# A graph network's dense first layer: the ELU split over ScalarE and VectorE another way, its output a step later

## Chip, cores and metric

The kernel runs on one core of one Trainium2 chip. The metric is the device time of one execution in microseconds (us): 4633.51 us is the median of three runs of the kernel before (4628.96 to 4634.05).

## What is computed

The program is a chain of four graph layers over 50000 nodes of 128 features and 12500 edges. Only the first layer matters here, and of it the part that every node takes:

```python
def _L0_gnn_ref(x, edge_index, edge_attr, u, batch, W1a, b1a, W1b, b1b, W2a, b2a, W2b, b2b):
    ...
    agg = summed / jnp.maximum(counts, 1.0)[:, None]
    z = jnp.concatenate([x, agg], axis=1)
    return jax.nn.elu(z @ W2a + b2a) @ W2b + b2b

x = _layernorm(x + _L0_gnn_ref(x, edge_index, edge_attr_128, ...), axis=-1)
```

Most nodes receive no edge, so for them `agg` is zero and the layer is x + ELU(x W2a[0:128] + b2a) W2b + b2b, normalised over its 128 features. The kernel computes this "dense" form for all nodes; the nodes with edges are computed again in a later stage. ELU(v) is v for v > 0 and exp(v) - 1 otherwise.

## The kernel before

All engines follow one list, `plan` (L512 to L527), written in Python before any instruction is issued. Each engine calls its own function for each entry of the list (`follow`, L529), so every engine has its work in the same order, and semaphores carry the data from one to the other. The list mixes two jobs:

- **The sort of the edges.** Edges are taken in 26 groups of 512. `hist` (26 entries) counts keys: VectorE makes one-hot matrices in bf16 (L770, L771), TensorE multiplies them (L645). `table` makes running sums and a node table in DRAM. `rank` (112 entries, called slots here, four to a group of edges) finds each edge's place: GpSimd (POOL) issues two indirect gathers per slot (`note`, L594) and two indirect scatters per slot (`place`, L601), TensorE looks up and counts (L678, L664), ScalarE makes one-hots by square and rectified line (L732, L735, L746, L749), VectorE compares, extracts and matches (L771, L851, L855, L840).
- **The dense layer.** The nodes are taken in 98 groups g of 512, four nodes to a partition. The entry `dense k` is one step of a software pipeline; `staged(k - lag, NG, f)` calls f for group k - lag.

Thirteen dense steps lie between the `hist` entries (one after each two), two behind `table`, and the other 88 are spread over the 112 slots, so that about four slots of five have a dense step behind them.

What each engine does in dense step k, in its own order:

- SP: load x of group k+1 (`load_x`, waits until POOL has used that buffer), load the transposed x of group k+2 (`load_xt`), store the result of group k-5 (`store1`).
- TensorE: `out0` of group k-2 (L697, eight 128x128 products into the one bank OUT0), then `hidden` of group k (L690, two products of 512 columns into two of three banks HB). `out0` waits for VectorE's `residual1` of group k-3, since there is one OUT0 bank, and VectorE does that in the same step k.
- ScalarE: `scale1` of group k-4 (L720, four normalising activations), then `exps` of group k (L712): exp(HB + b2a) into `hid1`, two activations of 128x512.
- VectorE: `shift` of group k-4 (L876), `elu_low` of group k-1 (L905), `residual1` of group k-3 (L882), `elu_high` of group k-1 (L910, two instructions), then `stats1`, `moments`, `eps` of group k-3 (L888, L895, L901).
- POOL: `add_bias` of group k-1 (L621, x + b2b into `xb`; waits for `residual1` of group k-3), then `power` of group k-3 (L627, the power -0.5 of the variance; waits for `eps` of group k-3, same step).

The ELU is done by these two functions of VectorE:

```python
def elu_low(g):
    after(dve, expd, g)
    nc.vector.tensor_scalar(hid1[g % 2][:, :, :], hid1[g % 2][:, :, :], 1.0, -1.0, MIN, ADD).then_inc(tmin, 1)

def elu_high(g):
    after(dve, tmin, g)
    for h in range(2):
        nc.vector.scalar_tensor_tensor(hid1[g % 2][:, h, :], HB[(2 * g + h) % 3][:, :], bias[h], hid1[g % 2][:, h, :], ADD, MAX).then_inc(elud, 1)
```

`after(eng, sem, g)` lets an engine wait until `sem` has been raised g+1 times. `hid1` and `xb` lie in SBUF, HB and OUT0 in PSUM. `after`, `after_ring` and `staged` are at L141 to L162, the block's LAST (the number of dense steps, 103) at L506.

Of the kernel before, what the change touches and what calls it, by code (L numbers as in the profile page):

```python
# [21 lines left out]
P = 128  # L22
# [142 lines left out]
def build(nc, a, out):  # L165
    ctx = ExitStack()
    with ctx:
# [53 lines left out]
        b2b_bc = sb("b2b_bc", [P, J, D])  # L221
        WL1 = sb("WL1", [P, D])
# [36 lines left out]
        hid = hid2[0]  # L259
        agg = [sb(f"agg{u}", [P, 2, GR]) for u in range(2)]  # L260
# [80 lines left out]
        with nc.Block() as block:  # L341
# [81 lines left out]
            def _(dve):  # L423
# [12 lines left out]
                nc.vector.tensor_tensor(b0[:, 6:8], b0[:, 4:6], B[0][:, 0:2], ADD).then_inc(floats, 1)  # L436
                dve.wait_ge(tpe, 3)
# [4 lines left out]
                dve.wait_ge(floats, 6)  # L442

            @block.tensor
            def _(pe):
                pe.wait_ge(made, 1)
                pe.wait_ge(raw_st, 1)
                for f in range(7):
                    if f >= 2:
                        pe.wait_ge(tpe, f - 1)  # L450
                    if f == 0:
# [6 lines left out]
                        for c in range(2):  # L458
                            for q in range(2):
                                last = nc.tensor.matmul(B[0][:, c:c + 1], W2a[:, 1 + q, c * P:(c + 1) * P], b0[:, 2 + q:3 + q],  # L460
                                                        start=(q == 0), stop=(q == 1))
                        last.then_inc(wf_p, 1)
# [6 lines left out]
         hidd, expd, tmin, elud, xbd, y1d, r1d, st1d, mvd, epsd, powd, shd, x1d) = ph.sems(33)  # L469
# [29 lines left out]
        HB, OUT0 = [PS[4], PS[5], PS[7]], PS[6]  # L499
        xd = [*x2N[0], spare_x]  # L500
        xt = [agg[u][:, h, :] for u in range(2) for h in range(2)]
        hid1 = hid2[0]
# [3 lines left out]
        LAST = NG + 5  # L506
# [33 lines left out]
        with nc.Block() as block:  # L540

            @block.sync
            def _(sp):
# [28 lines left out]
                def dense(k):  # L572
                    staged(k + 1, NG, load_x)
                    staged(k + 2, NG, load_xt)
                    staged(k - 5, NG, store1)

                load_x(0)
# [7 lines left out]
            def _(pool):  # L585
# [32 lines left out]
                def add_bias(g):  # L618
                    after_ring(pool, x_in, g, 16)
                    after(pool, r1d, g - 2)  # L620
                    nc.gpsimd.tensor_tensor(flat(xb[g % 2]), flat(xd[g % 3]), flat(b2b_bc), ADD).then_inc(xbd, 1)  # L621
# [16 lines left out]
            def _(pe):  # L638
# [47 lines left out]
                def hidden(g):  # L686
                    after_ring(pe, xt_in, g, 16)
                    for h in range(2):
                        after(pe, elud, 2 * g + h - 3)
                        nc.tensor.matmul(HB[(2 * g + h) % 3][:, :], W2a[:, 0, h * P:(h + 1) * P], xt[g % 4], start=True, stop=True).then_inc(hidd, 1)  # L690

                def out0(g):
                    after(pe, elud, 2 * g + 1)
                    after(pe, r1d, g - 1)
                    for j in range(J):
                        for c in range(2):
                            last = nc.tensor.matmul(OUT0[:, spans[j]], hid1[g % 2][:, c, spans[j]], W2b[:, c, :], start=(c == 0), stop=(c == 1))  # L697
# [9 lines left out]
            def _(act):  # L707
                def exps(g):
                    after(act, y1d, g - 2)
                    for h in range(2):  # L710
                        after(act, hidd, 2 * g + h)
                        last = nc.scalar.activation(hid1[g % 2][:, h, :], HB[(2 * g + h) % 3][:, :], ACT.Exp, bias=bias[h])  # L712
                    last.then_inc(expd, 1)
# [9 lines left out]
                def dense(k):  # L723
                    staged(k - 4, NG, scale1)
# [34 lines left out]
            def _(dve):  # L759
# [118 lines left out]
                def residual1(g):  # L878
# [3 lines left out]
                    nc.vector.tensor_tensor(flat(r1[g % 2]), OUT0[:, :], flat(xb[g % 2]), ADD).then_inc(r1d, 1)  # L882
# [20 lines left out]
                def elu_low(g):  # L903
                    after(dve, expd, g)
                    nc.vector.tensor_scalar(hid1[g % 2][:, :, :], hid1[g % 2][:, :, :], 1.0, -1.0, MIN, ADD).then_inc(tmin, 1)  # L905

                def elu_high(g):
                    after(dve, tmin, g)
                    for h in range(2):
                        nc.vector.scalar_tensor_tensor(hid1[g % 2][:, h, :], HB[(2 * g + h) % 3][:, :], bias[h], hid1[g % 2][:, h, :], ADD, MAX).then_inc(elud, 1)  # L910

                def dense(k):
                    staged(k - 4, NG, shift)
                    staged(k - 1, NG, elu_low)
                    staged(k - 3, NG, residual1)
                    staged(k - 1, NG, elu_high)
# [2336 lines left out]
```

## Time and profile before

| what | value |
|---|---|
| median of three runs | 4633.51 us |
| lowest, highest | 4628.96, 4634.05 us |
| the profiled execution, its own time | 4636.57 us |
| span of the profiled execution | 4634.4 us |
| mean granted TensorE clock | 0.916 |
| busy: PE, DVE, ACT, POOL | 3559.5, 3407.8, 2211.6, 3222.0 us |

The block that the change touches runs from about 36 us to 1000 us of the span: `hist` with its dense steps until about 165 us, `table` until about 184 us, then the slots. Blocks are one after the other, with all engines meeting at each end. Engines: PE is TensorE, PEld its weight load, DVE is VectorE, ACT is ScalarE, POOL is GpSimd, SP is the queue of plain transfers. A row of grouped instructions has busy time, mean duration in ns, then the idle time of the engine just before them and what ended it. A row of a timeline has start and duration in us; the bracket is idle time before it and what ended that. Neighbouring VectorE instructions overlap a little in their recorded times, so the pitch from start to start is the cost of one.

### The profile page before, as it was taken

How to read it: one execution, taken by the hardware profiler on the slowest of the kernel's cores; microseconds unless marked ns; L12 is line 12 of the kernel's file. 1: busy time of each engine (PE TensorE's matmuls, PEld its weight loads, DVE VectorE, ACT ScalarE, POOL GpSimd, SP SyncE). 2: the span in 40 equal slices, each digit the busy share in tenths (PEclk: the TensorE clock that was granted, in tenths of full speed). 3: DMA queues.
4: the chain of work that ended last, by engine and by line, in shares of the span. 5: the costliest groups of instructions: out<-in, count | busy, mean ns of one | idle time of the engine just before them, and what ended most of it. 6: DMA issues, size and time to landing. Idle time of an engine off the chain costs nothing. (4 is left out here: it accounts for less than half of the span.)

```text
span 4634.4 us, 61427 instructions
## 1 busy us (share of the span) xinstructions
PE 3559.5 (77%) x14977; PEld 2219.4 (48%) x14977; DVE 3407.8 (74%) x10458; ACT 2211.6 (48%) x4450; POOL 3222.0 (70%) x2802
## 2 busy tenths in 40 slices
PE   5677777747777566489979999998688758687975
PEld 3465555534444466444435555554343357564321
DVE  7777877755666688755546888888766669797964
ACT  1366666632333477623327777777122313123742
POOL 1377878757777588677747888888588766462557
PEclk9888989879999787799989999999899979898988
DMA  3344444432333467534433333333333258695863
GB/s 92 95 126 117 123 116 128 121 99 80 96 96 91 130 205 208 170 114 140 135 112 107 125 125 125 125 125 117 102 109 107 86 178 254 160 193 144 279 197 111
DMA packets 463592, 621.19 MB, mean 134 GB/s; under 512 B 71541, under 2 KB 220204, under 8 KB 463308
## 3 DMA queue, kind: packets, MB, share of 16 engines
q1 hardware_dynamic: 402700, 534.09, 37.1%
q0 software_dynamic: 54912, 83.37, 8.3%
q8 instruction: 105, 1.72, 0.2%
q10 hardware_dynamic: 5696, 0.55, 0.1%
q14 instruction: 179, 1.47, 0.1%
HBM read 402.95 MB, written 218.46 MB: 134 GB/s over the span
## 5 line engine op out<-in xcount | busy, mean ns | idle before, releaser
L1180 PE MATMUL ps<-big,Whh 128*128 128x512 f32 x1176 | 540.1, 595 | 33.5 <-DVE big L1198 30.9
L697 PE MATMUL ps<-W2b,hid 128*128 128x128 f32 x1568 | 249.3, 326 | 197.6 <-DVE rN L882 197.6
L1605 PE MATMUL ps<-big,We 128*128 128x512 f32 x800 | 356.2, 599 | 5.0 <-DVE big L1755 3.8
L697 PEld LDWEIGHTS ps<-W2b,hid 128*128 128x128 f32 x1568 | 236.4, 236 | 234.9 <-issue 233.1
L1180 PEld LDWEIGHTS ps<-big,Whh 128*128 128x128 f32 x1176 | 212.2, 190 | 254.3 <-issue 251.4
L1213 POOL TENSOR_TENSOR big<-big 128x512 f32<-128x512 f32 x196 | 251.6, 1303 | 73.0 <-ACT big L1207 73.0
L712 ACT ACTIVATE hid<-ps,b 128x512 f32<-128x512 f32 x196 | 134.0, 686 | 300.0 <-PE ps L690 290.0
L594 POOL DMA_INDIRECT me<-node_tab,ix x208 | 217.4, 1045 | 72.7 <-issue 52.8
L1755 DVE SCALAR_TENSOR_TENSOR big<-r2N,zN 128x512 f32<-128x512 f32 x400 | 252.7, 685 | 16.2 <-DMA r2N<-type_row 6.4
L601 POOL DMA_INDIRECT meta<-me,rank_ix x208 | 214.1, 1030 | 63.1 <-issue 60.6
L1605 PEld LDWEIGHTS ps<-big,We 128*128 128x128 f32 x800 | 151.5, 192 | 188.3 <-issue 182.5
L1198 DVE SCALAR_TENSOR_TENSOR big<-ps,bhh,hid 128x512 f32<-128x512 f32 x196 | 142.4, 744 | 125.9 <-ACT hid L1191 119.7
L1223 POOL TENSOR_TENSOR big<-big 128x512 f32<-128x512 f32 x98 | 141.3, 1462 | 127.3 <-DVE big L1218 127.3
L1527 POOL DMA_INDIRECT xN<-h_tab,ix x100 | 169.9, 1699 | 56.5 <-issue 28.8
L1121 DVE TENSOR_SCALAR zN<-rN,moments,rstd 128x128 f32<-128x128 f32 x392 | 191.7, 561 | 22.6 <-POOL rstd L1109 22.6
L2716 POOL DMA_INDIRECT xN<-x_tab,ix x100 | 161.6, 1616 | 67.2 <-PE ps L2730 35.4
L690 PE MATMUL ps<-agg,W2a 128*128 128x512 f32 x392 | 206.5, 654 | 0.0
L1190 ACT ACTIVATE hid<-ps,brz 128x512 f32<-128x512 f32 x196 | 134.6, 687 | 137.8 <-PE ps L1180 132.5
L678 PE MATMUL ps<-big,hotrow 128*128 128x256 f32 x832 | 188.5, 380 | 5.7 <-ACT hotrow L735 5.7
L2746 PEld LDWEIGHTS ps<-big,hid 128*128 128x128 f32 x1600 | 187.5, 194 | 8.0 <-DVE hid L2865 1.5
L2746 PE MATMUL ps<-big,hid 128*128 128x128 f32 x1600 | 189.6, 277 | 1.1 <-DVE hid L2865 1.1
L2418 ACT ACTIVATE hid<-big,shq,rsq 128x128 f32<-128x128 f32 x392 | 160.5, 483 | 31.9 <-DVE shq L2525 31.9
(403 smaller groups left out, 10744.3 us busy)
## 6 DMA issues: line engine op xcount, KB each, us to landing
xN<-x_tab SPq DMA_DIRECT2D x196, 256.0 KB, 3.0
h_tab<-yN SPq DMA_DIRECT2D x124, 256.0 KB, 2.3
krow<-key_row SPq DMA_DIRECT2D x100, 256.5 KB, 4.3
agg<-in_xt SPq DMA_DIRECT2D x98, 256.0 KB, 3.2
big<-x_tab SPq DMA_DIRECT2D x98, 256.0 KB, 3.1
x_tab<-hid SPq DMA_DIRECT2D x98, 256.0 KB, 3.5
agg<-x_tab SPq DMA_DIRECT2D x98, 256.0 KB, 2.8
x_tab<-zN SPq DMA_DIRECT2D x98, 256.0 KB, 2.0
```

What stands on the lines that cost most here:

```text
L594: nc.gpsimd.indirect_dma_start(me[:, t, f:f + 4], None, node_tab, at_index(which, i, j)).then_inc(noted[i % 2].sem, 16)
L601: nc.gpsimd.indirect_dma_start(meta[k], bass.IndirectOffsetOnAxis(ap=rank_ix[:, k, t:t + 1], axis=0), me[:, t, :], None).then_inc(stored[k ...
L678: last = nc.tensor.matmul(LOOK[j // 2][:, (j % 2) * LO:(j % 2 + 1) * LO], hotrow[k][:, h, j * P:(j + 1) * P], R[:, k, h, :], start=(h == 0 ...
L690: nc.tensor.matmul(HB[(2 * g + h) % 3][:, :], W2a[:, 0, h * P:(h + 1) * P], xt[g % 4], start=True, stop=True).then_inc(hidd, 1)
L697: last = nc.tensor.matmul(OUT0[:, spans[j]], hid1[g % 2][:, c, spans[j]], W2b[:, c, :], start=(c == 0), stop=(c == 1))
L1121: last = nc.vector.tensor_scalar(self.y[u][:, j, :], self.r[u][:, j, :], self.mv[u][:, j, 0:1], self.rs[u][:, j, :], SUB, MUL)
L1180: last = nc.tensor.matmul(bank[:, :], Whh[:, l, c * D:(c + 1) * D], h, start=True, stop=not both)
L1213: nc.gpsimd.tensor_tensor(self.d[u], h[u], self.n[u], SUB).then_inc(self.dd, 1)
L1527: nc.gpsimd.indirect_dma_start(xs[u][:, j, :], None, x2_e if l == 0 else h1_tab, at_index(IX_X2SRC if l == 0 else IX_H1SRC, g + EDGE0, j)) ...
L1605: last = nc.tensor.matmul(MS[:, :], We[:, l * NTYPE + t, :], masked[g % 2][:, t, :], start=(t == 0), stop=(t == NTYPE - 1))
L1755: last = nc.vector.scalar_tensor_tensor(masked[u][:, t, :], types[u], float(t), hs[u], EQ, MUL)
L2746: last = nc.tensor.matmul(OUT[u][:, spans[j]], ranked[u][m][:, spans[j]], weightI[l][m], start=(m == 0), stop=(m == TOP - 1))
```

## The change

The ELU is computed as min(exp(v), 1) + max(v, 0), which is ELU(v) + 1. ScalarE makes both parts from PSUM, with a second activation (Relu) for each half into a new buffer `above`; VectorE joins them by one `scalar_tensor_tensor` over 1024 columns with both inputs in SBUF. The extra 1 is taken back through the bias: `b2b_less` is b2b minus the column sums of W2b, made once in the setup block by two products with a matrix of ones (TensorE) and four subtractions (VectorE). ELU buffers become three, output banks OUT0 two, hidden banks HB two. The join moves from step g+1 to g+2, `out0` from g+2 to g+3, `residual1`, `stats1`, `moments`, `eps` and `power` from g+3 to g+4, `shift` and `scale1` from g+4 to g+5, the store from g+5 to g+6; `add_bias` moves from g+1 to g+3 and its load from g-1 to g. LAST goes from 103 to 104, so 89 dense steps are spread over the 112 slots.

```diff
+        b2b_less = sb("b2b_less", [P, J, D])
+        hid3 = [sb(f"hid_c{u}", [P, 2, GR]) for u in range(2)]
...
                 nc.vector.tensor_tensor(b0[:, 6:8], b0[:, 4:6], B[0][:, 0:2], ADD).then_inc(floats, 1)
+                for j in range(J):
+                    last = nc.vector.tensor_tensor(b2b_less[:, j, :], b2b_bc[:, j, :], H[1][0][:, 0:D], SUB)
+                last.then_inc(floats, 1)
...
+                        for c in range(2):
+                            last = nc.tensor.matmul(H[1][0][:, 0:D], ones[:, :], W2b[:, c, :], start=(c == 0), stop=(c == 1))
                         last.then_inc(wf_p, 1)
...
-        HB, OUT0 = [PS[4], PS[5], PS[7]], PS[6]
+        HB, OUT0 = PS[4:6], PS[6:8]
-        hid1 = hid2[0]
+        hid1, above = [*hid2[0], hid3[0]], [*hid2[1], hid3[1]]
-        LAST = NG + 5
+        LAST = NG + 6
...
                 def dense(k):
-                    staged(k + 1, NG, load_x)
+                    staged(k, NG, load_x)
                     staged(k + 2, NG, load_xt)
-                    staged(k - 5, NG, store1)
+                    staged(k - 6, NG, store1)
...
-                    nc.gpsimd.tensor_tensor(flat(xb[g % 2]), flat(xd[g % 3]), flat(b2b_bc), ADD).then_inc(xbd, 1)
+                    nc.gpsimd.tensor_tensor(flat(xb[g % 2]), flat(xd[g % 3]), flat(b2b_less), ADD).then_inc(xbd, 1)
...
                 def dense(k):
-                    staged(k - 1, NG, add_bias)
-                    staged(k - 3, NG, power)
+                    staged(k - 3, NG, add_bias)
+                    staged(k - 4, NG, power)
...
                     for h in range(2):
-                        after(pe, elud, 2 * g + h - 3)
-                        nc.tensor.matmul(HB[(2 * g + h) % 3][:, :], W2a[:, 0, h * P:(h + 1) * P], xt[g % 4], start=True, stop=True).then_inc(hidd, 1)
+                        after(pe, reld, 2 * g + h - 2)
+                        nc.tensor.matmul(HB[h][:, :], W2a[:, 0, h * P:(h + 1) * P], xt[g % 4], start=True, stop=True).then_inc(hidd, 1)
 
                 def out0(g):
-                    after(pe, elud, 2 * g + 1)
-                    after(pe, r1d, g - 1)
+                    after(pe, elud, g)
+                    after(pe, r1d, g - 2)
...
                 def dense(k):
-                    staged(k - 2, NG, out0)
+                    staged(k - 3, NG, out0)
                     staged(k, NG, hidden)
...
                 def exps(g):
-                    after(act, y1d, g - 2)
+                    after(act, y1d, g - 3)
+                    after(act, elud, g - 3)
                     for h in range(2):
                         after(act, hidd, 2 * g + h)
-                        last = nc.scalar.activation(hid1[g % 2][:, h, :], HB[(2 * g + h) % 3][:, :], ACT.Exp, bias=bias[h])
-                    last.then_inc(expd, 1)
+                        nc.scalar.activation(hid1[g % 3][:, h, :], HB[h][:, :], ACT.Exp, bias=bias[h])
+                        nc.scalar.activation(above[g % 3][:, h, :], HB[h][:, :], ACT.Relu, bias=bias[h]).then_inc(reld, 1)
...
-                    staged(k - 4, NG, scale1)
+                    staged(k - 5, NG, scale1)
                     staged(k, NG, exps)
...
-                def elu_low(g):
-                    after(dve, expd, g)
-                    nc.vector.tensor_scalar(hid1[g % 2][:, :, :], hid1[g % 2][:, :, :], 1.0, -1.0, MIN, ADD).then_inc(tmin, 1)
-
-                def elu_high(g):
-                    after(dve, tmin, g)
-                    for h in range(2):
-                        nc.vector.scalar_tensor_tensor(hid1[g % 2][:, h, :], HB[(2 * g + h) % 3][:, :], bias[h], hid1[g % 2][:, h, :], ADD, MAX).then_inc(elud, 1)
+                def elu(g):
+                    after(dve, reld, 2 * g + 1)
+                    nc.vector.scalar_tensor_tensor(hid1[g % 3][:, :, :], hid1[g % 3][:, :, :], 1.0, above[g % 3][:, :, :], MIN, ADD).then_inc(elud, 1)
 
                 def dense(k):
-                    staged(k - 4, NG, shift)
-                    staged(k - 1, NG, elu_low)
-                    staged(k - 3, NG, residual1)
-                    staged(k - 1, NG, elu_high)
-                    staged(k - 3, NG, stats1)
-                    staged(k - 3, NG, moments)
-                    staged(k - 3, NG, eps)
+                    staged(k - 5, NG, shift)
+                    staged(k - 2, NG, elu)
+                    staged(k - 4, NG, residual1)
+                    staged(k - 4, NG, stats1)
+                    staged(k - 4, NG, moments)
+                    staged(k - 4, NG, eps)
```

VectorE, one dense step among the slots, between an extract (L851, L855; in the change L858, L862) and what follows. Before:

```order
L855 TENSOR_TENSOR big<-big,ps 128x512 [waits odd14]
...
L876 SCALAR_TENSOR_TENSOR shq<-mvq,rsq 128x4 [waits odd32,odd30]
L905 TENSOR_SCALAR hid<-hid 128x1024 [waits odd21]
L882 TENSOR_TENSOR rN<-ps,xb 128x512 [waits odd32,odd24,odd25]
L910 SCALAR_TENSOR_TENSOR hid<-ps,b,hid 128x512 [waits odd22]
L910 SCALAR_TENSOR_TENSOR hid<-ps,b,hid 128x512
L888 BN_STATS stats<-rN 128x6 [waits odd28,odd26]
```

In the change:

```order
L862 TENSOR_TENSOR big<-big,ps 128x512 [waits odd14]
...
L883 SCALAR_TENSOR_TENSOR shq<-mvq,rsq 128x4 [waits odd31,odd29]
L912 SCALAR_TENSOR_TENSOR hid_c<-hid_c 128x1024 [waits odd21]
L889 TENSOR_TENSOR rN<-ps,xb 128x512 [waits odd31,odd23,odd24]
L895 BN_STATS stats<-rN 128x6 [waits odd27,odd25]
```

The three ELU instructions have become one of 1024 columns, directly behind `shift` (L883), and nothing stands between `residual1` and `stats1` now.

POOL, the first dense instructions, in the `hist` part. Before (L621 is `add_bias`, L627 is `power`):

```order
L621 TENSOR_TENSOR xb<-xN,b2b_bc 128x512 x2
L621 TENSOR_TENSOR xb<-spare_x,b2b_bc 128x512
L627 TENSOR_TENSOR rsq<-veq,mhalf 128x4
L621 TENSOR_TENSOR xb<-xN,b2b_bc 128x512
L627 TENSOR_TENSOR rsq<-veq,mhalf 128x4
```

In the change (L627 is `add_bias`, L633 is `power`):

```order
L627 TENSOR_TENSOR xb<-xN,b2b_less 128x512 x2
L633 TENSOR_TENSOR rsq<-veq,mhalf 128x4
L627 TENSOR_TENSOR xb<-spare_x,b2b_less 128x512
L633 TENSOR_TENSOR rsq<-veq,mhalf 128x4
L627 TENSOR_TENSOR xb<-xN,b2b_less 128x512
```

The two alternate as before, but an `add_bias` no longer waits for a `residual1` of its own step: the one that it waits for was done a step earlier.

## Rows read from the trace of the kernel before

**Rows 1.** The page's part on busy time, whole program.

```profile
span 4634.4 us, 61427 instructions
PE 3559.5 (77%) x14977; PEld 2219.4 (48%) x14977; DVE 3407.8 (74%) x10458; ACT 2211.6 (48%) x4450; POOL 3222.0 (70%) x2802
```

**Rows 2.** Busy time by stretch: length, then PE, PEld, DVE, ACT, POOL, granted clock, DMA.

```profile
36.00:155.00 119.00, 91.51 (x591) 60.75 (x592) 117.50 (x518) 28.30 (x54) 24.20 (x22) 1.00 0.24 77
220.00:900.00 680.00, 523.59 (x2545) 404.33 (x2544) 542.84 (x2063) 447.62 (x805) 539.86 (x502) 0.89 0.44 122
937.00:1000.00 63.00, 39.42 (x214) 31.14 (x212) 42.89 (x173) 32.75 (x64) 42.30 (x40) 0.88 0.24 73
```

**Rows 3.** Waits of 220 to 900 us: who for whom, us, times, longest.

```profile
ACT hid L712 <- PE ps L690: 195.3, 72, 5.2
PE ps L697 <- DVE rN L882: 154.3, 43, 5.6
DVE hid L905 <- ACT hid L712: 51.7, 38, 3.0
POOL rsq L627 <- DVE veq L901: 25.0, 28, 1.4
POOL xb L621 <- DVE rN L882: 9.9, 6, 2.1
```

**Rows 4.** Groups of instructions, 220 to 900 us.

```profile
L594 POOL DMA_INDIRECT me<-node_tab,ix x185 | 193.7, 1047 | 48.7 <-issue 46.9 <-DMA me<-node_tab,ix 0.9 <-ACT yN L720 0.6
L601 POOL DMA_INDIRECT meta<-me,rank_ix x173 | 178.7, 1033 | 52.7 <-issue 50.6 <-ACT yN L720 0.9 <-DVE rank_ix L866 0.6
...
L712 ACT ACTIVATE hid<-ps,b 128x512 f32<-128x512 f32 x144 | 98.3, 686 | 202.5 <-PE ps L690 195.3
...
L627 POOL TENSOR_TENSOR rsq<-veq,mhalf 128x4 f32<-128x4 f32 x72 | 77.6, 1078 | 27.7 <-DVE veq L901 25.0
```

**Rows 5.** POOL's indirect DMAs singly, 220 to 900 us: shortest, median, longest ns.

```profile
L594 POOL DMA_INDIRECT me<-node_tab,ix x185: 941/987/1506, 219.4 to 898.3; - x185
L601 POOL DMA_INDIRECT meta<-me,rank_ix x173: 982/998/1505, 258.2 to 899.6; - x173
```

**Rows 6.** Timeline of POOL, one slot with its dense step.

```profile
554.38 1.49 POOL L594 DMA_INDIRECT me<-node_tab,ix  x1 [0.20 <-issue]
556.17 0.97 POOL L594 DMA_INDIRECT me<-node_tab,ix  x1 [0.30 <-issue]
...
559.77 1.28 POOL L621 TENSOR_TENSOR xb<-xN,b2b_bc 128x512 f32<-128x512 f32 x1
561.00 1.04 POOL L627 TENSOR_TENSOR rsq<-veq,mhalf 128x4 f32<-128x4 f32 x1
562.23 1.50 POOL L594 DMA_INDIRECT me<-node_tab,ix  x1 [0.20 <-issue]
```

**Rows 7.** Timeline of VectorE in the same slot.

```profile
562.07 0.16 DVE L876 SCALAR_TENSOR_TENSOR shq<-mvq,rsq 128x4 f32<-128x4 f32 x1 [3.00 <-POOL rsq L627]
562.15 0.69 DVE L905 TENSOR_SCALAR hid<-hid 128x1024 f32<-128x1024 f32 x1
```

**Rows 8.** Timeline, POOL and VectorE, an edge match (L840) against an indirect DMA.

```profile
217.68 1.41 POOL L594 DMA_INDIRECT me<-node_tab,ix  x1 [0.19 <-issue]
...
217.46 0.75 DVE L840 SCALAR_TENSOR_TENSOR big<-xT,ef,mask 128x512 f32<-128x512 f32 x1
```

**Rows 9.** Timeline of VectorE, a dense step among the `hist` entries.

```profile
150.62 0.68 DVE L905 TENSOR_SCALAR hid<-hid 128x1024 f32<-128x1024 f32 x1
151.22 0.68 DVE L882 TENSOR_TENSOR rN<-ps,xb 128x512 f32<-128x512 f32 x1
151.82 1.40 DVE L910 SCALAR_TENSOR_TENSOR hid<-ps,b,hid 128x512 f32<-128x512 f32 x2
153.14 0.86 DVE L888 BATCH_NORM_STATS2 stats<-rN 128x6 f32<-128x128 f32 x4
```

**Rows 10.** Timeline, POOL's `add_bias` against VectorE's one-hots in `hist`.

```profile
45.20 1.29 POOL L621 TENSOR_TENSOR xb<-xN,b2b_bc 128x512 f32<-128x512 f32 x1 [1.75 <-DMA xN<-in_x]
...
45.22 1.36 DVE L771 TENSOR_SCALAR big<-iota_lo,ef 128x256 bf16<-128x256 bf16 x1
46.50 0.28 DVE L770 TENSOR_SCALAR big<-iota_lo,ef 128x256 bf16<-128x256 bf16 x1
```

**Rows 11.** A join of two SBUF inputs elsewhere in the program, and output products.

```profile
L2854 DVE SCALAR_TENSOR_TENSOR yN<-krow,spare_win 128x512 f32<-128x512 f32 x34 | 23.3, 684 | 0.0
...
L697 PE MATMUL ps<-W2b,hid 128*128 128x128 f32 x1568 | 249.3, 326 | 197.6 <-DVE rN L882 197.6
```

More of the change, by code:

```diff
@@ L441, in _ @@
                 nc.vector.memset(inv_e[:, :], 1.0).then_inc(floats, 1)
-                dve.wait_ge(floats, 6)
+                dve.wait_ge(floats, 7)
             @block.tensor
@@ L468, in build @@
         (hoth, histd, cum, tot, off, offs, start_, tabs, own_d, has_d, map_d, hot, hotT, looked, counted, based, eqd, radd, base_w, ranked,
-         hidd, expd, tmin, elud, xbd, y1d, r1d, st1d, mvd, epsd, powd, shd, x1d) = ph.sems(33)
+         hidd, reld, elud, xbd, y1d, r1d, st1d, mvd, epsd, powd, shd, x1d) = ph.sems(32)
         tab_st, mv_set, squared, squared_hi, hot_hi = ph.sems(5)
@@ L572, in dense @@
                 def dense(k):
-                    staged(k + 1, NG, load_x)
+                    staged(k, NG, load_x)
                     staged(k + 2, NG, load_xt)
-                    staged(k - 5, NG, store1)
-                load_x(0)
+                    staged(k - 6, NG, store1)
                 load_xt(0)
@@ L688, in hidden @@
                     for h in range(2):
-                        after(pe, elud, 2 * g + h - 3)
-                        nc.tensor.matmul(HB[(2 * g + h) % 3][:, :], W2a[:, 0, h * P:(h + 1) * P], xt[g % 4], start=True, stop=True).then_inc(hidd, 1)
+                        after(pe, reld, 2 * g + h - 2)
+                        nc.tensor.matmul(HB[h][:, :], W2a[:, 0, h * P:(h + 1) * P], xt[g % 4], start=True, stop=True).then_inc(hidd, 1)
                 def out0(g):
-                    after(pe, elud, 2 * g + 1)
-                    after(pe, r1d, g - 1)
+                    after(pe, elud, g)
+                    after(pe, r1d, g - 2)
                     for j in range(J):
                         for c in range(2):
-                            last = nc.tensor.matmul(OUT0[:, spans[j]], hid1[g % 2][:, c, spans[j]], W2b[:, c, :], start=(c == 0), stop=(c == 1))
+                            last = nc.tensor.matmul(OUT0[g % 2][:, spans[j]], hid1[g % 3][:, c, spans[j]], W2b[:, c, :], start=(c == 0), stop=(c == 1))
                     last.then_inc(y1d, 1)
                 def dense(k):
-                    staged(k - 2, NG, out0)
+                    staged(k - 3, NG, out0)
                     staged(k, NG, hidden)
@@ L881, in residual1 @@
                     after(dve, x1d, g - 2)
-                    nc.vector.tensor_tensor(flat(r1[g % 2]), OUT0[:, :], flat(xb[g % 2]), ADD).then_inc(r1d, 1)
+                    nc.vector.tensor_tensor(flat(r1[g % 2]), OUT0[g % 2][:, :], flat(xb[g % 2]), ADD).then_inc(r1d, 1)
                 def stats1(g):
```

## The prediction

> **What bounds the kernel now.** The page's busy times [rows 1] only say that no engine is alone in front: PE 77%, DVE 74%, POOL 70% of the whole program. The change touches one block of it, so I cut that block into stretches [rows 2]. In 36 to 155 us, the `hist` part, DVE is busy 117.5 of 119 us: it is the bound, and whatever it sheds there is gained. In 220 to 900 us, 92 slots with 72 dense steps, DVE is busy 543 of 680 us, PE 524, ACT 448 and POOL 540: nobody is full. Next I look at who waits for whom there [rows 3]. The large waits (ACT for `hidden` 195 us, PE for `residual1` 154 us, DVE for `exps` 52 us) form the ring that the change cuts. But POOL waits for DVE for only 25.0 + 9.9 = 34.9 us. The rest of its idle time stands in the groups [rows 4] as "issue": 46.9 + 50.6 us, the 0.3 us in front of each indirect DMA, which nothing shortens. So POOL works or issues for 680 - 34.9 = 645 us, 95% of the stretch. **POOL is the floor**, and cutting the ring between the others can give back 34.9 us there at most.
>
> One more thing must be read before the sum. An undelayed indirect DMA takes about 0.98 us, and some take 1.5 [rows 5]. The timeline shows when: POOL ends a `power`, DVE's `shift` was waiting for it and starts at 562.07, L905 follows at 562.15, and POOL's next DMA, begun at 562.23, lasts until 563.73, where the next ones take 0.97 [rows 6, 7]. L905 ended at 562.84. A DMA of that kind therefore waits for the end of a VectorE instruction that came before its own first access, and that costs it 0.48 us. It is the same with an instruction that has two SBUF inputs: the match that ran from 217.46 to 218.21 makes the DMA begun at 217.68 last 1.41 us [rows 8].
>
> **The change, part by part.**
>
> *Setup.* PE makes two more products ahead of the semaphore on which ACT and the transposes wait. Eight of them take 16 records; back to back one product costs about 0.25 us, and the mean record is 326 ns [rows 11]. I take **+0.5 us** (0.5 to 1.3). The four subtractions on DVE are small and fall into a wait for ACT; were that cover gone, they would cost about 1 us.
>
> *The hist part.* DVE sheds L905 (pitch 0.60) and two L910 (pitch together 1.32) [rows 9], 1.92 us in 12 steps = 23.0. It gains the join: 512 columns from two SBUF inputs take 684 ns [rows 11], of which some 0.15 us is fixed as between the pitches above, so 1024 columns have a pitch of 1.13 us (bounds: 1.05 and twice 0.68 = 1.37) in 11 steps = 12.4. A set of `residual1` to `eps` (2.0 us) leaves the part with the later step. With nothing between `residual1` and `stats1`, the semaphore shows, 0.12 us in 9 steps. In all 23.0 + 2.0 - 12.4 - 1.1 = 11.5 us less.
> But `add_bias` loses its cover. Before, it was released by `residual1` and ran under L910, which reads PSUM and one SBUF input and was not slowed. Now it follows the `power` of the step before at once and meets DVE's one-hots. The trace has that meeting: `add_bias` from 45.20 to 46.49, and the one-hot begun at 45.22 takes 1.36 instead of 0.28 us [rows 10]. That is 1.08 us in 8 steps = 8.6 us back. Net **-3 us** (0 to -11.5).
>
> *The slots, 220 to 900 us.* (a) POOL's waits for DVE go: `add_bias` now waits for a step-old result, and `eps` is ready about 3.4 us after `power` of the step before, where POOL needs some 7 us to come back: **-34.9**. (b) 89 steps instead of 88 in the same slots, 0.8 of a step of POOL's two operations here: **+2**. (c) The delays by L905 go. DMAs lose 185 x 0.060 + 173 x 0.035 = 17 us to DVE over their medians [rows 4, 5]; the rest of it is the match's, about a third: **-12**. (d) The join's own delays come. POOL being the floor, DVE will nearly always stand at `shift` when `power` ends, as at 562.07, where it had waited 3.00 us. Then the join starts 0.08 us before the DMA and ends about 1.13 us behind its start, where L905 ended at 0.61 and cost 0.48: 1.0 us each time. A match in front of it makes DVE late now and then. Bounds: 1.0, and 0.5 if its place were random between DMAs that start 1.3 us apart. I take 0.95, since the row at 562 has DVE waiting: 73 x 0.95 = **+69** (36 to 73). Together **+24 us** (-9 to +28).
>
> *The other slots.* Before 220 us POOL only gathers, and in the last twelve (937 to 1000 us) it only scatters, and is busy 42.3 of 63 us [rows 2]: there it has slack, and the cut ring gives something. At 1.3 us a DMA and 2.35 + 1.0 us a dense step the last twelve need about 57 us: **-5 us** for both ends (0 to -12).
>
> *What is hidden.* The added Relu, 2 x 0.69 us a step [rows 4], comes to 100 us of ACT in the stretch: 448 + 100 = 548 of some 700 us, hidden under POOL. If POOL were not the floor, it would be ACT's turn: with `scale1`, both pairs and the edge work it has about 7.3 us in a slot with a dense step, and POOL 7.4. Now `hidden` has two banks, so PE waits for ACT's read; it has over half a step to spare. `load_xt` now stands behind a `load_x` that waits for the `add_bias` of the same step; the data is wanted two steps later. `scale1` and the store a step later cost nothing, as x1 keeps three buffers.
>
> Sum: 0.5 - 3 + 24 - 5 = **+16.5 us**. The profiled execution took 4636.6 us for a span of 4634.4, so it becomes 4653; it lies 3.1 us above the median, and the prediction for the median is 4633.5 + 16.5 = **4650 us**.
>
> The Trainium skill, "SBUF — State Buffer", section "Who interferes with whom", says that a VectorE instruction with two SBUF inputs contends with a GpSimd instruction that reads SBUF, the second one blocking until the first is done; by that rule the join costs as in (d), and the match row agrees. The same section infers that such an instruction leaves descriptor generation alone, since that wants the write interface; by this, (d) would be nothing.
>
> **The rivals.**
>
> *The join misses the DMAs (faster).* POOL loses the waits, and DVE arrives at the join at changing places. The point from which it decides is the mean delay d of a step: 0.5 - 3 - 5 - 34.9 + 2 - 12 + 73 d is zero at d = 0.72 us. At 0.5 it gives 4633.5 - 16 = 4617. For it: only nine or so of 72 dense steps show the 1.49 us DMA now. Against: that is because DVE is late in this kernel, and it will be early.
>
> *No delay from a join (faster).* Descriptor work might wait only for L905, which reads one tensor and runs 1024 columns in 0.69 us. POOL's floor is then 600 us, and ACT with its 548 us and its waits for `hidden` comes next; I put the stretch at about 640 to 645, so -40 with the ends: 4590 to 4595. That is the skill's inference as a mechanism here. Against it stands the match row [rows 8].
>
> *ACT and PE become the ring (slower still).* With two HB banks, `hidden` waits for the Relu of the step before, and ACT for `hidden`, with a lookup and count of edges on PE between. If that takes over 8.4 us a dense slot, POOL's new pace, it decides; 0.5 us more in 89 steps gives 4650 + 40 = 4690, and half of it 4670.
>
> *It cancels (no change).* The delays take what the waits gave, d between 0.6 and 0.85, or `power` keeps some wait for `eps`: 4633 +- 9.
>
> **How the numbers follow.** The forecast (join in front of the DMA, 4643 to 4668) gets 0.46; cancelling 0.24; join missing the DMAs 0.17; no delay 0.07; the ACT and PE ring 0.06. About 0.2% or 9.3 us is what a measurement of this kernel can tell from no change. Slower by more is most of the forecast and the ring, 0.49; faster by more is both faster rivals and an edge of cancelling, 0.27; within 0.24. The range 4608 to 4668 holds the forecast with its bounds and the first rival's 4617, and leaves out the 4590s and the ring. The forecast's own range is 4643 to 4668.
>
> **What the changed profile would show.** Right: POOL's waits for DVE in the slots fall from 34.9 to under 8 us; `shift` waits for `power` in most steps; the join takes about 1.2 us and starts just before POOL's first DMA, which then takes about 2.0 us, so that the mean of the gathers rises from 1.05 to 1.25 us or more; ACT near 78% busy; in the `hist` part one one-hot a step lasts about 1.3 us. Wrong: gathers that keep their mean near 1.05 us, or a median near 0.98 with few above 1.5; ACT or PE busy above 90%; or PE idle before `hidden`, waiting for the Relu.

## The result and the profile after

| | median | lowest to highest |
|---|---|---|
| before, 20 runs | 4631.65 us | 4622.28 to 4640.45 |
| after, 20 runs | 4625.43 us | 4618.30 to 4633.27 |

The ratio is 0.9985, 95% interval 0.9978 to 0.9992: some 6 us faster, which is real and under the 0.2% that the prediction called no change. It lies inside the range (4608 to 4668). The most likely case, slower by 16.5 us, did not come; the case "it cancels" did.

The page's busy times after, which answer to [rows 1]:

```profile
span 4623.5 us, 61438 instructions
PE 3566.6 (77%) x14981; PEld 2223.2 (48%) x14981; DVE 3389.5 (73%) x10266; ACT 2313.3 (50%) x4646; POOL 3256.4 (70%) x2802
```

Fixed windows can't say where 6 us went, because the same slot lies at another time in each kernel. So here the block is cut at events, and each row gives the length, then busy time of PE, PEld, DVE, ACT, POOL. The cuts: VectorE's copy of `me` (just ahead of `hist`), the first gather, the first scatter (slot 8), the last gather (slot 99), the end of the last scatter. Before:

```profile
33.64:184.01 150.37, 106.27 (x668) 71.39 (x669) 145.19 (x612) 35.17 (x70) 27.86 (x26) 0.95 0.23 75
184.01:258.24 74.23, 52.83 (x244) 39.39 (x242) 50.49 (x196) 44.41 (x82) 47.76 (x45) 0.83 0.49 139
258.24:935.63 677.39, 516.97 (x2496) 398.46 (x2497) 537.22 (x2039) 440.80 (x792) 543.25 (x505) 0.89 0.43 120
935.63:999.49 63.86, 40.79 (x226) 32.38 (x224) 43.74 (x174) 34.12 (x66) 43.63 (x41) 0.88 0.26 80
```

After:

```profile
36.05:185.11 149.06, 108.82 (x666) 74.02 (x667) 141.83 (x574) 49.46 (x96) 24.09 (x23) 0.94 0.21 70
185.11:251.05 65.94, 49.46 (x251) 36.14 (x250) 52.11 (x181) 52.16 (x99) 50.69 (x45) 0.88 0.48 143
251.05:934.21 683.16, 522.50 (x2547) 401.06 (x2546) 518.62 (x1914) 520.77 (x948) 579.03 (x508) 0.87 0.41 121
934.21:993.55 59.34, 32.95 (x172) 26.95 (x171) 43.94 (x158) 31.83 (x63) 47.54 (x42) 0.76 0.29 91
```

Ahead of the first cut +2.4 us, `hist` and `table` -1.3, the first eight slots -8.3, slots 8 to 99 +5.8, the last twelve -4.5: together -5.9. The rest of the span's difference (10.9) lies in later blocks that the change leaves alone. In slots 8 to 99 VectorE is busy 18.6 us less and POOL 35.8 us **more**, with the same operations but for one more dense step: an expected gain was given back on POOL.

The waits of 220 to 900 us after, against [rows 3]:

```profile
DVE shq L883 <- POOL rsq L633: 140.7, 38, 7.0
PE ps L703 <- DVE rN L889: 85.5, 21, 7.4
ACT hid L719 <- PE ps L696: 15.4, 6, 2.9
POOL rsq L633 <- DVE veq L908: 4.0, 1, 4.0
```

The ring is cut: ACT's wait for `hidden` fell from 195 to 23 us (the 15.4 shown and 8.0 under the buffer's other name `hid_c`), and POOL's wait of 25.0 + 9.9 to 4.0. VectorE now waits for POOL. The groups of the same stretch, against [rows 4], and the gathers singly, against [rows 5]:

```profile
L600 POOL DMA_INDIRECT me<-node_tab,ix x184 | 226.3, 1230 | 47.7 <-issue 45.6 <-DMA me<-node_tab,ix 1.5 <-DVE rank_ix L873 0.3
L607 POOL DMA_INDIRECT meta<-me,rank_ix x174 | 177.5, 1020 | 53.0 <-issue 47.6 <-DVE rank_ix L873 4.9 <-DMA me<-node_tab,ix 0.6
L912 DVE SCALAR_TENSOR_TENSOR hid<-hid 128x1024 f32<-128x1024 f32 x49 | 59.5, 1215 | 0.0
```

```profile
L600 POOL DMA_INDIRECT me<-node_tab,ix x184: 943/990/2050, 220.5 to 896.0; - x184
```

The gathers' mean rose from 1047 to 1230 ns while their median stayed at 990: a minority is twice as long. The timelines of POOL and of VectorE (start, duration) show which. First a step in which VectorE stood waiting at `shift`:

```profile
569.53 1.04 POOL L633 TENSOR_TENSOR rsq<-veq,mhalf 128x4 f32<-128x4 f32 x1
570.77 2.04 POOL L600 DMA_INDIRECT me<-node_tab,ix  x1 [0.19 <-issue]
573.11 0.97 POOL L600 DMA_INDIRECT me<-node_tab,ix  x1 [0.30 <-issue]
...
570.61 0.16 DVE L883 SCALAR_TENSOR_TENSOR shq<-mvq,rsq 128x4 f32<-128x4 f32 x1 [2.58 <-POOL rsq L633]
570.69 1.22 DVE L912 SCALAR_TENSOR_TENSOR hid<-hid 128x1024 f32<-128x1024 f32 x1
```

The join starts 0.08 us ahead of the gather and ends at 571.91; the gather ends 0.90 us after that and has lost 1.02 us. This is term (d) as the prediction drew it. Then a step that it did not draw:

```profile
539.49 1.28 POOL L627 TENSOR_TENSOR xb<-xN,b2b_less 128x512 f32<-128x512 f32 x1
540.73 1.24 POOL L633 TENSOR_TENSOR rsq<-veq,mhalf 128x4 f32<-128x4 f32 x1
542.17 1.02 POOL L600 DMA_INDIRECT me<-node_tab,ix  x1 [0.20 <-issue]
...
538.74 2.32 DVE L847 SCALAR_TENSOR_TENSOR big<-xT,ef,mask 128x256 f32<-128x256 f32 x1
...
541.54 0.74 DVE L847 SCALAR_TENSOR_TENSOR big<-xT,ef,mask 128x512 f32<-128x512 f32 x1
542.21 0.15 DVE L883 SCALAR_TENSOR_TENSOR shq<-mvq,rsq 128x4 f32<-128x4 f32 x1
542.29 1.21 DVE L912 SCALAR_TENSOR_TENSOR hid<-hid 128x1024 f32<-128x1024 f32 x1
```

A match of 256 columns met POOL's `add_bias` and took 2.32 us instead of the usual 0.48, so VectorE reached `shift` late; the join came 0.12 us after the gather's start and the gather took 1.02 us. The match ends 0.29 us after `add_bias` does. It began 0.75 us ahead of it, while a scatter was being issued, and why it was still open when `add_bias` came is not shown. I sorted the 72 steps of slots 8 to 99 by the join's start after the end of `power`: up to 0.2 us in 41 steps, whose first gather averages 2.03 us; 0.3 to 0.4 us in 16 steps, 1.02 us; 0.4 to 0.8 us in 5 steps, 1.41 us; later in 10. So VectorE was late in 31 steps, and in 21 of these a match of 256 columns had been stretched to 2.06 to 2.34 us. The joins hold 53 DMAs in all, and their delays add up to 45.4 us, 0.63 a step. The break-even of the prediction was 0.72.

### The profile page after: what moved, and what is told of

It reads as the page before. It is cut to its first block and busy times, and to the rows that moved or that the text cites. A ratio compares the mean times of both kernels' runs of the same rounds, so it can differ in the third digit from the quotient of the medians.

```text
span 4623.5 us, 61438 instructions
## 1 busy us (share of the span) xinstructions
PE 3566.6 (77%) x14981; PEld 2223.2 (48%) x14981; DVE 3389.5 (73%) x10266; ACT 2313.3 (50%) x4646; POOL 3256.4 (70%) x2802
## 5 line engine op out<-in xcount | busy, mean ns | idle before, releaser
L600 POOL DMA_INDIRECT me<-node_tab,ix x208 | 255.8, 1230 | 71.1 <-issue 51.7
L684 PE MATMUL ps<-big,hotrow 128*128 128x256 f32 x832 | 212.6, 414 | 30.2 <-issue 22.4
L1528 POOL DMA_INDIRECT xN<-h_tab,ix x100 | 170.3, 1703 | 56.5 <-issue 28.8
L703 PE MATMUL ps<-W2b,hid 128*128 128x128 f32 x1056 | 151.5, 305 | 73.9 <-DVE rN L889 73.8
L684 PEld LDWEIGHTS ps<-big,hotrow 128*128 128x128 f32 x832 | 172.2, 211 | 72.9 <-issue 37.2
L696 PE MATMUL ps<-agg,W2a 128*128 128x512 f32 x392 | 197.0, 626 | 3.8 <-ACT hid L720 3.8
L703 PEld LDWEIGHTS ps<-W2b,hid 128*128 128x128 f32 x1056 | 146.7, 218 | 91.0 <-DVE hid L912 85.4
L633 POOL TENSOR_TENSOR rsq<-veq,mhalf 128x4 f32<-128x4 f32 x98 | 108.1, 1103 | 110.6 <-DVE veq L908 109.1
```

Of the source, the lines that this page charges most:

```text
L600: nc.gpsimd.indirect_dma_start(me[:, t, f:f + 4], None, node_tab, at_index(which, i, j)).then_inc(noted[i % 2].sem, 16)
L684: last = nc.tensor.matmul(LOOK[j // 2][:, (j % 2) * LO:(j % 2 + 1) * LO], hotrow[k][:, h, j * P:(j + 1) * P], R[:, k, h, :], start=(h == 0 ...
L696: nc.tensor.matmul(HB[h][:, :], W2a[:, 0, h * P:(h + 1) * P], xt[g % 4], start=True, stop=True).then_inc(hidd, 1)
L703: last = nc.tensor.matmul(OUT0[g % 2][:, spans[j]], hid1[g % 3][:, c, spans[j]], W2b[:, c, :], start=(c == 0), stop=(c == 1))
L1528: nc.gpsimd.indirect_dma_start(xs[u][:, j, :], None, x2_e if l == 0 else h1_tab, at_index(IX_X2SRC if l == 0 else IX_H1SRC, g + EDGE0, j)) ...
```

## The experiments

Ratios are to runs of the kernel before on the same chip: it takes 4633 to 4635 us there, and 4707.65 us on a second chip, on which three of the kernels were measured (it is said at each) and the changed kernel was not. "Excess" is the time that the indirect DMAs of slots 8 to 99 took over their undelayed 1.02 us (the first after `power`), 0.96 (gather) or 0.99 us (scatter), summed: 19.0 us before, 52.0 after.

**A spacer.** A small memset between `shift` and the join, of 128 columns and later of 320, in the changed kernel:

```diff
+        gap = sb("gap", [P, 128])
...
                     nc.vector.scalar_tensor_tensor(shq[q][:, 0:J], moment(q)[:, :, 0], -1.0, rsq[q][:, 0:J], MUL, MUL).then_inc(shd, 1)
+                    nc.vector.memset(gap[:, :], 0.0)
```

> The changed kernel with one VectorE memset of 128 columns (some 0.19 us) between shift and the join, so that a join behind a waited-for shift starts about 0.30 us after POOL's power and not 0.11. Theory (place): POOL's first indirect DMA, issued 0.20 us after power, makes its access before 0.31 us; the 41 DMAs of 2.03 us fall to 1.02, the gathers' mean from 1.23 to about 1.03 us, and the kernel gains about 1.0 us in some 45 steps: about 4580 us. Rival (share): what counts is how long VectorE holds the port, 1.2 us a step as before; then the mean of the gathers stays near 1.2 and the time near 4625. Rival (next floor): the gathers fall but ACT or PE takes over, and only half arrives: about 4603.

Measured: 4633.45 us, ratio 0.999 (0.9981 to 0.9999); excess 56.5 us. No gain came. The join came only 0.14 us later, which is 0.05 us after the gather's start, and the 41 gathers took 2.11 us.

> The memset of s1_gap at 320 columns. In s1_gap the join moved only to 0.25 us behind power (0.05 behind the start of the DMA), the first DMAs took 2.11 us, 0.08 more than before, as the join ended 0.08 later: the DMA still lost. In the changed kernel the 16 joins at 0.31 to 0.36 us left the DMA at 1.02. With 320 columns the join should start at 0.32 to 0.36. Theory (place decides, the edge lies between 0.25 and 0.31 us): first DMAs of 1.02, second ones 0.96 to 1.00, DMA excess in slots 8 to 99 from 52 to 12 us, time about 4625 - 42 = 4583. Rival (next floor): excess falls but the time stays above 4600. Rival (share of the port): excess stays near 50, 4625 to 4635.

Measured: 4645.73 us, ratio 1.0031 (1.0019 to 1.0043); excess 70.9 us. POOL and VectorE there:

```profile
580.57 2.31 POOL L601 DMA_INDIRECT me<-node_tab,ix  x1 [0.19 <-issue]
...
580.41 0.16 DVE L884 SCALAR_TENSOR_TENSOR shq<-mvq,rsq 128x4 f32<-128x4 f32 x1 [2.58 <-POOL rsq L634]
580.59 0.33 DVE L885 MEMSET gap<- 128x320 f32 x1
580.83 1.16 DVE L914 SCALAR_TENSOR_TENSOR hid<-hid 128x1024 f32<-128x1024 f32 x1
```

The join starts 0.26 us after the gather and the gather loses all the same: it ends 0.89 us after the join's end (581.99). Against my theory of places at first sight. What runs at the gather's first access is the memset, so it looks as if the memset held the gather off and the join took over without a gap; that is argued, not shown. A memset is then no neutral spacer, and the theory needs a neutral one.

**`residual1` between `shift` and the join**, an instruction that reads PSUM and one SBUF tensor:

```diff
                     staged(k - 5, NG, shift)
-                    staged(k - 2, NG, elu)
                     staged(k - 4, NG, residual1)
+                    staged(k - 2, NG, elu)
```

> The changed kernel with residual1 between shift and the join: the join starts about 0.71 us after power and ends at 1.85, so the first DMA (access before 0.31) is free and the second one (begun at 1.52) waits until 1.85. Place theory: first DMAs 1.02, second ones about 1.35, 0.35 us a step instead of 1.0 in the steps where shift waited: about 4598 us. Share rival: no change, 4625.

Measured: 4610.02 us, ratio 0.9944 (0.9931 to 0.9957); excess 38.1 us: 12 us above the place theory's time, and well below the 4625 of the other. First gathers 1.02 us, second ones 1.28 us where `shift` had waited: the join starts 0.75 us after the end of `power` and still runs when the second gather begins.

**The join ahead of `shift`**, so that it no longer starts right when `power` ends and lets both `shift` and the next DMA go:

```diff
-                    staged(k - 5, NG, shift)
                     staged(k - 2, NG, elu)
+                    staged(k - 5, NG, shift)
                     staged(k - 4, NG, residual1)
```

> The changed kernel with the join before shift, so that it does not wait for power and runs behind the edge work at changing places. Place theory: delays of 0 to 1.1 us spread over all four DMAs of a slot, 0.4 to 0.5 us a step on average against 0.62 now: about 4612 us (4600 to 4622). Share rival: 4625.

Measured: 4594.68 us, ratio 0.9908 (0.9893 to 0.9924), 31 us below the changed kernel; excess 24.8 us, slots 8 to 99 656.68 us instead of 683.16. That is better than the 4600 to 4622 expected. The gathers of 220 to 900 us have the mean of the kernel before again:

```profile
L600 POOL DMA_INDIRECT me<-node_tab,ix x190 | 198.9, 1047 | 49.4 <-issue 44.9 <-DMA me<-node_tab,ix 2.6 <-ACT yN L727 1.2
```

The join has not moved under `power`: of the 72 joins in slots 8 to 99 none lies wholly under it. Nine begin there and run into the gather, 5 begin 0.07 to 0.08 us ahead of a DMA and cost it 1.0 us each, and 58 begin inside a DMA or with it, and do nothing to that one; 20 of these still run when the next DMA starts. In all 34 DMAs are held, for 16.1 us instead of 45.4. What changed is that the join rarely starts just ahead of a DMA now. One of the 58, with the match in front of it:

```profile
526.36 1.02 POOL L600 DMA_INDIRECT me<-node_tab,ix  x1 [0.20 <-issue]
...
525.72 0.74 DVE L847 SCALAR_TENSOR_TENSOR big<-xT,ef,mask 128x512 f32<-128x512 f32 x1
...
526.40 1.22 DVE L912 SCALAR_TENSOR_TENSOR hid<-hid 128x1024 f32<-128x1024 f32 x1
```

**The neutral spacer.** The first 128 columns of `residual1` ahead of the join, the other 384 behind it:

```diff
+                    nc.vector.tensor_tensor(r1[g % 2][:, 0, :], OUT0[g % 2][:, 0:D], xb[g % 2][:, 0, :], ADD)
...
                     staged(k - 5, NG, shift)
+                    staged(k - 4, NG, residual1)
                     staged(k - 2, NG, elu)
-                    staged(k - 4, NG, residual1)
+                    staged(k - 4, NG, residual1b)
```

> The changed kernel with residual1 cut in two: its first 128 columns (PSUM and one SBUF input, about 0.2 us) stand between shift and the join, the other 384 behind the join, which raises the semaphore. VectorE's work is the same but for one instruction's fixed part (0.06 to 0.1 us a step). It gives the join the place that the two memsets were meant to give it (about 0.3 us behind the end of power), with a kind of instruction under which the trace shows DMAs of 1.02 us. Place theory (a DMA loses only to a join that starts ahead of the DMA's first access): in most of the 73 steps the first gather takes 1.02 to 1.05 us and the second 0.97; the DMAs' delays in slots 8 to 99 fall from 52 us to 12 to 20 and the time from 4625 to 4585 to 4595, as with the join first. Rival (the access lies later than 0.1 us behind the DMA's begin, or the join takes the port whenever it starts within the DMA's first half): first gathers stay at 2.1 us and the time at 4620 to 4640.

Measured, on a chip where the kernel before takes 4707.65 us: 4666.5 us, ratio 0.9912 (0.9897 to 0.9928); excess 21.2 us. POOL and VectorE:

```profile
584.20 1.02 POOL L600 DMA_INDIRECT me<-node_tab,ix  x1 [0.20 <-issue]
585.52 0.96 POOL L600 DMA_INDIRECT me<-node_tab,ix  x1 [0.30 <-issue]
...
584.03 0.16 DVE L883 SCALAR_TENSOR_TENSOR shq<-mvq,rsq 128x4 f32<-128x4 f32 x1 [6.45 <-POOL rsq L633]
584.14 0.29 DVE L889 TENSOR_TENSOR rN<-ps,xb 128x128 f32<-128x128 f32 x1
584.35 1.22 DVE L915 SCALAR_TENSOR_TENSOR hid<-hid 128x1024 f32<-128x1024 f32 x1
```

The join still lies on top of the gather, but for the gather's first 0.15 us, where it began 0.08 us ahead of it before: no delay. Slots 8 to 99 took 651.63 us, 31.5 less than in the changed kernel, with an excess 30.8 less. That is the price of the join's place. The changed kernel was traced on another chip, but that does not touch this: less their excess, slots 8 to 99 take 630.4 us here, 631.2 in the changed kernel and 631.1 to 632.9 in the four kernels of the experiments above, so the excess alone moves them.

**The join in two halves**, in place:

```diff
-                    nc.vector.scalar_tensor_tensor(hid1[g % 3][:, :, :], hid1[g % 3][:, :, :], 1.0, above[g % 3][:, :, :], MIN, ADD).then_inc(elud, 1)
+                    for h in range(2):
+                        last = nc.vector.scalar_tensor_tensor(hid1[g % 3][:, h, :], hid1[g % 3][:, h, :], 1.0, above[g % 3][:, h, :], MIN, ADD)
+                    last.then_inc(elud, 1)
```

> The changed kernel with the join as two instructions of 512 columns each, in place. The pitch of both is 1.2 to 1.3 us (twice about 0.63) against 1.13. If a DMA waits only for the VectorE instruction that holds the port at its access, and gets in between two instructions, the first gather of the 41 steps with DVE early takes about 1.5 us instead of 2.03 and the second half then hits nothing or the late part of the same DMA: the delays fall from 52 to 25 to 35 us and the time to 4600 to 4612. If back-to-back instructions leave no gap for the DMA, it waits for both: 2.1 us, and the time is 4628 to 4640. Each of the two readings bears on what the memset in front of the join did.

Measured on the same chip as the last: 4675.9 us, ratio 0.9937 (0.9923 to 0.9951); excess 31.4 us. The 41 early gathers took 1.50 us:

```profile
586.80 1.49 POOL L600 DMA_INDIRECT me<-node_tab,ix  x1 [0.20 <-issue]
...
586.72 1.28 DVE L913 SCALAR_TENSOR_TENSOR hid<-hid 128x512 f32<-128x512 f32 x2
```

The gather waits for one instruction, not for the pair, as the first of the two readings said. Slots 8 to 99 less their excess are 631.5 us again. Between two joins it gets in, where between memset and join it did not.

**The new ELU on the old schedule**: ScalarE's Relu, the join and the bias, with one OUT0 bank, three HB banks and all steps as before:

```diff
-                    staged(k - 1, NG, elu_low)
+                    staged(k - 1, NG, elu)
                     staged(k - 3, NG, residual1)
-                    staged(k - 1, NG, elu_high)
...
```

> The new ELU alone (Exp and Relu by ScalarE, one join by VectorE, b2b less the column sums) on the schedule of the kernel before: join at step g+1, one output bank, three hidden banks, two ELU buffers, add_bias at g+1. Theory: POOL still waits for residual1 and eps of the same step, 20 to 35 us in the slots, and the joins lie at changing places and cost DMAs about 0.5 us each: 4630 to 4655 us, 4640 the likeliest. The hist part gets shorter by 0.8 us a step, since add_bias keeps its place. Rival: the shorter VectorE alone is what gives, and this is at 4615 or below.

Measured: 4694.37 us, ratio 1.0124 (1.0109 to 1.0139), well above the 4630 to 4655 expected. Waits of 220 to 900 us:

```profile
ACT hid L719 <- PE ps L696: 173.6, 64, 5.8
PE ps L703 <- DVE rN L889: 168.1, 52, 6.1
DVE hid L912 <- ACT hid L720: 122.7, 43, 5.3
POOL xb L627 <- DVE rN L889: 79.1, 40, 4.6
```

With the ring uncut, two Relus lengthen it; the wait passes from VectorE on to POOL (9.9 before, 79.1 here), and slots 8 to 99 take 723.41 us, though the DMAs' excess is only 18.4. So the later steps are worth about 69 us to the new ELU (4694.37 against 4625.43 us), even with the 45.4 us of join delays that they bring. In `hist`, where `add_bias` keeps its old cover here, it took 144.44 us, 5.9 less than before.

**`add_bias` in `hist`.** In the changed kernel it is made to wait there for the `residual1` of the same dense step, as it did before the change:

```diff
-                    after(pool, r1d, g - 2)
+                    after(pool, r1d, g - 1 if g + 3 < EG // 2 else g - 2)
```

> The changed kernel where add_bias in the steps among the hist entries waits for residual1 of the group before (same step), as in the kernel before, and so runs beside stats1 and not beside the one-hots. Theory: the one one-hot of 1.38 us in each of these steps falls to 0.28, a step from 10.69 to about 9.6 us, the hist part 9 us shorter: about 4616 us. Rival: another wait takes it, TensorE's dense products in front of the hist products: under 3 us.

Measured: 4611.51 us, ratio 0.9955 (0.9943 to 0.9967); `hist` and `table` 138.12 us:

```profile
33.95:172.07 138.12, 105.76 (x666) 72.60 (x667) 131.74 (x574) 49.38 (x96) 24.26 (x22) 0.93 0.23 75
```

The other slots are as in the changed kernel (65.94 and 682.92 us). The reverse, the kernel before with `add_bias` one step later alone:

```diff
-                    staged(k - 1, NG, add_bias)
+                    staged(k - 2, NG, add_bias)
```

> The kernel before with add_bias alone a step later (g+2), so that it waits for no result of its own step. Theory: in the hist part it meets the one-hots, 1.1 us in 8 steps, +9 us; in the slots POOL loses its 10 us of waits for residual1, but it then waits longer for eps, since the ring between the others stays: 0 to -10 there. 4630 to 4640, no clear difference to the kernel before. Rival: the waits for residual1 were real, and it gains 10 us or more in all.

Measured: 4657.09 us, ratio 1.0051 (1.0038 to 1.0064); `hist` and `table` 159.43 us, 9.1 more. Slots 8 to 99 took 4 us more, the first eight 6.5 and the last twelve 5.7, which I had not expected and whose cause is open. What the two show together: the meeting of `add_bias` with the one-hots is real in either kernel. One-hots that take 1.36 us or more in `hist`: 1 in the kernel before and 10 with its `add_bias` later; 10 in the changed kernel and 1 with the wait. In the changed one, POOL and VectorE:

```profile
103.33 1.50 POOL L627 TENSOR_TENSOR xb<-xN,b2b_less 128x512 f32<-128x512 f32 x1
...
103.54 1.38 DVE L778 TENSOR_SCALAR big<-iota_lo,ef 128x256 bf16<-128x256 bf16 x1
104.84 0.27 DVE L777 TENSOR_SCALAR big<-iota_lo,ef 128x256 bf16<-128x256 bf16 x1
```

**Both mends together.** First the join ahead of `shift` with the wait in `hist`, then the quarter of `residual1` with it:

> Join before shift (s3) and the hist wait (s6) together, the version meant to beat both kernels. Theory: both gains add, 4625 - 31 - 9 = 4585 us. Rival: they share a cause and only the larger one stays, 4595.

Measured: 4583.67 us, ratio 0.989 (0.9876 to 0.9904).

> The same with add_bias of the hist part waiting for the residual1 of one step earlier, which was worth 10.9 us there (149.1 to 138.1 us) when done alone. In that part the split costs one fixed part in 11 steps, about 1 us. If the two places are independent, the time is 10 to 14 us below that of the quarter residual alone: 4572 to 4583 by the place theory, 4607 to 4628 by the rival. If the cut instruction lets the waits meet again (add_bias under a later one-hot), the hist part stays at 149 us.

Measured, on the chip with 4707.65 us before: 4655.06 us, ratio 0.989 (0.9875 to 0.9906); `hist` and `table` 138.91 us. The two are equal within their intervals, and 1.1% below the kernel before: both beat before and after. The join first is the simpler edit.

## Why the prediction was wrong in its sign

*What bounds the kernel.* Right. POOL's waits for VectorE went nearly as term (a) said, from 34.9 to 4.0 us in 220 to 900 us; measured between the cuts of slots 8 to 99, the gaps in front of `add_bias` and `power` fell by 32.0 us, and nothing but POOL's own work took their place. ACT was busy 527.27 us in 220 to 900 (78% foretold, 77.5% found) and never became the bound; PE did not wait for the Relu for more than a few us.

*Term (d), the join's delays: the step that failed.* The mechanism was right: in 41 steps the first gather takes 2.03 us, 2.0 foretold. Its frequency was not: I took 0.95 us in each of 73 steps, +69, and it was 45.4 us, 0.63 a step. "POOL being the floor, DVE will nearly always stand at `shift` when `power` ends" was drawn from the one step at 562 us. The waits after show it in 38 of 73 steps. In the others VectorE was late, and one reason was in the trace of before, in [rows 10]: a large POOL instruction holds up a VectorE instruction that meets it. I used that for `hist` and not for the matches in the slots, where 21 of the 31 late steps have it. The bounds of 36 to 73 held the value, and my choice near their upper end turned the sign: 23.6 us of an error of 22.4, the other terms nearly cancelling. The rival "it cancels" had asked for a delay between 0.6 and 0.85 us a step, and that is what came.

*Term (c)*, -12: the excess fell by 12.4 us outside the joins. Right. *Term (b)*, +2: `add_bias` and `power` take 5.1 us more between the cuts (90.9 + 76.5 before, 92.2 + 80.3 after). The step more is 2.4 of it. The rest is `power` itself, whose mean rose from 1078 to 1116 ns; the prediction left that at nothing, and it takes 1.25 instead of 1.04 us in the steps with the stretched match. With that, slots 8 to 99 close: -32.0 + 45.4 - 12.4 + 5.1 = +6.1 against +5.8 measured.

*The ends*, -5 us, 0 to -12: -12.8, just outside. The last twelve slots gave 4.5, as reckoned from POOL's floor there. For the first eight I reckoned nothing, though POOL only gathers there and the ring set the pace; they gave 8.3. With the new ELU on the old schedule these eight take 85.67 us against 65.94, so it is the cut ring that gives it.

*`hist`*, -3: -1.3. Its two halves were both a little small: without the meeting the part is 12.2 us shorter than before (11.5 foretold), and the meeting costs 10.9 us (8.6 foretold, as 1.08 us in 8 steps). *Setup*, +0.5 with 1.3 as upper end: the two products (four records) take 1.20 us and all of it is on the path, since VectorE's wait ends with them:

```profile
33.19 1.20 PE L468 MATMUL ps<-W2b,ones 128*128 128x128 f32 x4
...
34.43 0.16 DVE L438 TENSOR_TENSOR b<-b,ps 128x2 f32<-128x2 f32 x1 [6.38 <-PE ps L468]
```

From there to the copy of `me` it is 1.62 us in both kernels, so the subtractions are hidden as said. The other 1.2 us of the later start comes before the products, in the loading of weights; that time differs by as much between the other runs (the copy starts between 33.4 and 35.9 us in the other kernels with the same setup).

The errors add up: (d) -23.6, the rest of slots 8 to 99 +5.4, ends -7.8, `hist` +1.7, all ahead of it +1.9 make -22.4, and 16.5 - 22.4 is the -5.9 us of the block.

*What the profile was to show.* POOL's waits under 8 us (4.0), a gather's 2.0 us, a one-hot's 1.3 us (1.38) and ACT's share came. `shift` waiting for `power` in most steps did not, and the gathers' mean stopped at 1.23 us where 1.25 or more was foretold. Those two were the signs of the frequency.

*The skill's rule.* Here the trace decides. The 41 gathers of 2.03 us under a join with two SBUF inputs speak against the inference of the Trainium skill, "SBUF — State Buffer", section "Who interferes with whom", that such an instruction leaves descriptor generation alone; by it the prediction put the changed kernel at 4590 to 4595 us. That time was itself not what the rows give. The rival's floor for POOL, 600 us, does not follow from its terms: 680 - 34.9 + 2 - 12 is 635, and the kernels above show 630 to 633 in slots 8 to 99 less the excess. Without the 45.4 us of join delays the changed kernel would be near 4580 us, an estimate. The kernel with the join first keeps 16.1 us of these delays, which fits its 4595 us.

## What to carry to other kernels

When an instruction's cost depends on where it falls against another engine, count over many steps where it falls; do not take the one step that shows the mechanism best. A work-shedding edit can be right and yet show nothing until its new instruction is placed: here moving one call up by a line gave 31 us, where the whole change gave 6. And when POOL issues indirect DMAs all the time, see that the end of a POOL instruction does not release a long VectorE instruction with SBUF inputs and the next DMA together, the VectorE instruction first. One short instruction that reads PSUM and one SBUF input, put between them, was enough here, and so was the join ahead of the wait.

## What the runs showed of the hardware

- Whether the join holds an indirect DMA is decided at the DMA's start. A join begun 0.08 us before the start costs the DMA 1.02 us; one begun 0.12 us after it (12 steps of the changed kernel) or 0.15 us after it costs nothing, though it covers all the rest. A held DMA ends 0.83 to 0.92 us after the end of the VectorE instruction (0.90 at 570.77 after, 0.89 at 580.57 in the kernel with the wide memset, 0.89 at 562.23 before), and an undelayed one takes 1.02 us. So an instruction that runs at the start but ends within 0.12 us of it costs nothing either, like the match at 525.72 above.
- The old ELU's L905, one SBUF input in 0.69 us, has a second hold that the join never shows. Thirteen DMAs of slots 8 to 99 in the kernel before, with L905 begun 0.34 to 0.55 us after their start, took 0.16 to 0.37 us more and ended 0.12 us after L905. With L905 begun 0.61 us after the start or later none did. Joins begun 0.55 to 0.57 us after a gather's start left it at 1.02 us (`residual1` between, 45 steps). One of the thirteen:

```profile
289.08 1.23 POOL L601 DMA_INDIRECT meta<-me,rank_ix  x1 [0.30 <-issue]
...
289.49 0.69 DVE L905 TENSOR_SCALAR hid<-hid 128x1024 f32<-128x1024 f32 x1 [1.30 <-ACT hid L712]
```

- A held DMA gets in between two joins of 512 columns (1.50 us instead of 2.03) but not between a memset and a join (2.11 and 2.31 us). Why a memset differs is open; no run took the memset apart from the join.
- Contention runs both ways: while VectorE holds POOL's DMAs, a one-hot that meets POOL's `add_bias` (1.28 us, 1.50 there) takes 1.38 us instead of 0.28, and a match of 256 columns 2.06 to 2.34 us instead of 0.48. `power` takes 1.25 instead of 1.04 us behind such a match.
